# Expert routing of a two-layer transformer: VectorE's placing chain in single steps, its running count as a scan, and layer 2's first sorted rows transposed behind the first weight copies

## The reference, cut to what matters

```python
x = L0_attn_x                                              # (4, 512, 128) float32, 4 batches of 512 tokens
for layer in (0, 1):                                       # written out twice in the source
    sa, ca, ga, sb, cb, gb = modulation of silu(c) @ wmod  # |ga| and |gb| at least 0.25
    h = _layernorm(x) * (1 + ca) + sa
    x = x + ga * attention(h)       # layer 0: causal, 16 heads of 8
                                    # layer 1: full attention, then two rounds over past states, then a gate
    h = _layernorm(x) * (1 + cb) + sb
    x = x + gb * experts(h)
# experts of layer 0: top 1 of 8
logits = einsum('btd,ed->bte', xn, gate_w);  top1_idx = argmax(softmax(logits));  top1_score = max(softmax(logits))
for e in range(8):
    h = silu(xn @ W1[e] + b1[e]);  ye = h @ W2[e] + b2[e];  out = where(top1_idx == e, ye, out)
out = out * top1_score
# experts of layer 1: top 2 of 8
logits = xf @ Wg;  top_v, top_i = top_k(logits, 2);  top_w = softmax(top_v)
y[e] = (silu(xf @ W1[e]) * (xf @ W3[e])) @ W2[e]           # e = 0..7, 512 hidden columns
out = y[top_i[:, 0]] * top_w[:, 0] + y[top_i[:, 1]] * top_w[:, 1]
```

## Time and profile before

| | us |
|---|---|
| median of 3 runs | 929.11 (927.58 to 929.59) |
| profiled execution | 929.22 |
| its span in the trace | 927.5 |
| PE busy | 855.9 (92%) |
| DVE busy | 741.7 (80%) |
| ACT busy | 586.8 (63%) |
| POOL busy | 279.5 (30%) |

### The profile page before, as it was taken

How to read it: one execution, slowest core, us unless ns; L and a number is a source line. 1 busy time by engine, 2 the same in 40 slices (tenths; PEclk the granted TensorE clock), 3 DMA queues, 4 the chain that set the end, 5 groups by cost and what they waited for, 6 DMA issues and landing times.

```text
span 927.5 us, 19266 instructions
## 1 busy us (share of the span) xinstructions
PE 855.9 (92%) x6883; PEld 543.1 (59%) x6883; DVE 741.7 (80%) x2162; ACT 586.8 (63%) x1277; POOL 279.5 (30%) x419
## 2 busy tenths in 40 slices
PE   8899999887878899999999999999999999989994
PEld 7556666554478874445444544445453344978993
DVE  6888888887457678988989887987989885787674
ACT  2457576655556526898889877878776685433331
POOL 6123232436411436403210110200105422445332
PEclk9899999999989999999999999999997897989997
DMA  4324410001012214700000000000080100102123
GB/s 137 107 61 140 112 46 23 21 19 43 14 42 81 56 35 155 238 1 2 2 1 2 2 1 2 1 1 2 1 273 30 43 1 9 51 24 77 53 71 106
DMA packets 47927, 48.38 MB, mean 52 GB/s; under 512 B 5606, under 2 KB 39398, under 8 KB 47576
## 3 DMA queue, kind: packets, MB, share of 16 engines
q1 hardware_dynamic: 39784, 38.03, 14.0%
q0 software_dynamic: 3296, 6.82, 2.3%
q10 hardware_dynamic: 4752, 2.30, 0.8%
HBM read 30.83 MB, written 21.02 MB: 56 GB/s over the span
## 4 chain that ended last, share of the span: by engine, by line
PE 59%; DVE 28%; POOL 4%; issue 4%; DMA 2%; ACT 2%; DVEq 0%; SPq 0%; POOLq 0%; ACTq 0%
PE pv L1728 14%; PE st L1705 9%; DVE M L2029 8%; PE ring L1696 7%; PE ring L1597 5%; PE ring L1842 4%; DVE ring L2033 4%; PE st L1597 4%; PE st L1827 3%; DVE M L2036 2%; PE ring L1658 2%; PE ring L1608 2%; PE st L1820 1%; POOL Xd L1313 1%; PE st L1835 1%
## 5 line engine op out<-in xcount | busy, mean ns | idle before, releaser
L1454 ACT ACTIVATE Et<-st 128x512 f32<-128x512 f32 (+3 forms) x768 | 374.0, 550 | 124.0 <-PE st L1705 120.1
L2036 DVE TENSOR_REDUCE M<-ring 128x1 f32<-128x512 f32 x256 | 159.6, 682 | 26.3 <-PE ring L1696 26.2
L2029 DVE TENSOR_REDUCE M<-ring 128x2 f32<-128x512 f32 x256 | 159.3, 680 | 15.9 <-PE ring L1696 15.8
L2033 DVE CUSTOM_DVE_ANT_0 ring<-ring,maskw 128x128 f32<-128x128 f32 (+3 forms) x256 | 121.3, 509 | 25.6 <-PE ring L1696 23.9
L1728 PE MATMUL pv<-Et,Va 128*32 128x256 f32 (+3 forms) x1536 | 136.4, 416 | 1.9 <-POOL Et L1268 1.9
L1696 PE MATMUL ring<-Kbd,Qa 128*128 128x128 f32 (+3 forms) x256 | 89.1, 369 | 9.0 <-DVE M L2033 5.7
L1268 POOL TENSOR_SCALAR_AFFINE_SELECT Et<-Et 128x256 f32<-128x256 f32 x128 | 53.3, 418 | 139.3 <-ACT Et L1454 137.6
L1728 PE MATMUL pv<-Et,RV 128*32 128x256 f32 x1024 | 88.7, 419 | 1.0 <-ACT PVs L1461 1.0
L1705 PE MATMUL st<-Qb,Kbd 128*128 128x512 f32 (+3 forms) x256 | 84.5, 351 | 5.0 <-ACT Et L1454 5.0
L1696 PE MATMUL ring<-RKT,Qa 32*128 32x512 f32 x256 | 80.8, 517 | 5.1 <-DVE M L2029 3.4
L1705 PE MATMUL st<-Qb,RKT 32*128 32x512 f32 x256 | 76.6, 523 | 0.0
(11 more groups left out here) (293 smaller groups left out, 1519.0 us busy)
## 6 DMA issues: line engine op xcount, KB each, us to landing
Xd<-Xd SPq DMA_DIRECT2D x8, 1056.0 KB, 16.0
L1W<-in_L1W SPq DMA_DIRECT2D x2, 2048.0 KB, 12.3
Kbd<-Ksb SPq DMA_DIRECT2D x60, 64.0 KB, 2.0
Xs<-Xd SPq DMA_DIRECT2D x39, 66.0 KB, 1.9
W<-in_L0W SPq DMA_DIRECT2D x8, 258.0 KB, 3.8
W<-in_L0W SPq DMA_DIRECT2D x8, 256.0 KB, 4.2
G<-Zd SPq DMA_DIRECT2D x8, 256.0 KB, 4.6
Yd<-Yt ACTq DMA_DIRECT2D x30, 64.0 KB, 1.5
```

The source lines that it names most:

```text
L1454: e.activation(Et[s // 2 % 4][:, j % 2, q0:512], bank(ph)[:, q0:512], ACT.Exp, scale=SCALE).then_inc(exp_done, 1)
L2029: e.tensor_reduce(M[i][:, t, j, :], bank(ph)[:, :].rearrange("p (two n) -> p two n", two=2), AX.X, ALU.max).then_inc(mx_red, 1)
L2033: e.tensor_tensor_reduce(bank(ph)[:, 0:n], bank(ph)[:, 0:n], maskw[:, 512 - n:512], 1.0, -3e38, ALU.add, ALU.max, M[i][:, t, j, 0:1]).then ...
L2036: e.tensor_reduce(M[i][:, t, j, 0:1], bank(ph)[:, 0:n], AX.X, ALU.max).then_inc(mx_red, 1)
```

## The change

1. Routing is cut into single-instruction phases. In the parts (layer 0, q=0), (layer 0, q=1) and (layer 1, q=0) a step is left between them, so that they alternate with VectorE's other work; in the other parts they follow each other as before, or with what does not depend on them between. The phases `tally` to `used` become a list that is spread over the scatters' steps.
2. The running count: the copy of `tot` and the 8 (or 4) chained additions become one copy from PSUM straight into `carry` (now stored by expert, with the start value ahead of each expert's counts) and one `tensor_tensor_scan` over 72 (40) elements, with a constant `joined` that is 0 at each expert's start. A second copy takes the ranks out of PSUM, and the addition reads them from SBUF. The start value of `carry` is set in `hot`.
3. In layer 1 the pair of multiply, reduce and cast for the two choices becomes one of double size: three operations fewer in each part.
4. POOL sets the constants of the scan at its start: four small MEMSETs ahead of `onesM`.
5. Layer 1, part q=0: `route` moves from the list at half pace to the one at full pace, so its scatters stand 2 steps apart, not 4; `getx` and `meta` of the first chunk stand behind the four `getw`, not ahead of them.

In steps of the plan (a unit has 16), layer 1's part q=0 moves as follows: `hot` 440 to 443, `rank` 444 to 447, `pos` 448 to 453, the scatters from 452-480 to 455-469, `used` from 484 to 469-471, `loadx` 484 to 480, `getx` 490 to 499, the four `getw` from 490, 495, 500, 505 to 480, 485, 490, 495. In layer 0, part q=0: `rank` 228 to 233, `pos` 234 to 246, the scatters from 236-250 to 248-262, `loadx` 252 to 264 and `getx` 258 to 270; part q=1: `pos` 265 to 277, its scatters from 267-273 to 279-285, and layer 0's first `getw` stay at 271, 276 and 281.

```diff
     def route(l, q):
+        busy = 1 if l + q < 2 else 0
         for i in range(l + 1):
-            for part in ("top", "topi"):
-                do(part, l, q, i)
-                yield from wait(1 if q < 2 else 0)
+            for k in range(6 if i < l else 5):
+                do("top", l, q, i, k)
+                yield from wait(busy or (q < 2 and k in (1, 4)))
         do("hot", l, q)
+        yield from wait(4 if busy else 2 if q < 2 else 1)
+        do("rank", l, q)
         yield from wait(2 if q < 2 else 1)
-        for part in ("rank", "pos") if l else ("rank", "tiles", "room", "pos"):
-            do(part, l, q)
-            yield from wait(2 if q < 2 else part in ("rank", "pos"))
-            if l and part == "rank":
-                do("wts", l, q)
+        do("carry", l, q)
+        if l:
+            do("wts", l, q, 0)
+        yield from wait(busy)
+        do("ranked", l, q)
+        if l:
+            do("wts", l, q, 1)
+        yield from wait(busy)
...
+        for k in range(2):
+            do("place", l, q, k)
+            if l:
+                do("wts", l, q, 2 + k)
+            yield from wait(busy)
+        do("pos", l, q)
+        yield from wait(2 if q < 2 else 1)
...
+        pace = 1 if busy else -(-len(chain) // (TILES_OF[q] * SPREAD[l][q]))
         for n in range(TILES_OF[q]):
             do("scatter", l, q, n)
-            if l and n < 4:
-                do(("tally", "scan", "choose", "eid")[n], l, q)
-            yield from wait(SPREAD[l][q])
...
+            for _ in range(SPREAD[l][q]):
+                for ph in chain[:pace]:
+                    do(*ph)
+                del chain[:pace]
+                yield
+        for ph in chain:
+            do(*ph)
+            yield
...
     def first_tokens(l):
...
-        yield from wait(6)
-        do("getx", l, 0)
-        if l:
-            do("meta", 0)
+        if l == 0:
+            yield from wait(6)
+            do("getx", l, 0)
         while ("shifted", l, LAST_USE[l]) not in flags:
             yield
         for n in range(NF if l else LEAD):
             yield from wait(5 if n else 0)
             do("getw", l, n)
+        if l:
+            yield from wait(4)
+            do("getx", l, 0)
+            do("meta", 0)
...
-    prep += [(at["rows", 0], token_rows(1, 0)), (at["route", 0], in_turn(token_rows(1, 1), route(1, 0))),
-             (at["weights"], layer1_weights()), (at["past"], past_prep())]
+    prep += [(at["rows", 0], token_rows(1, 0)), (at["weights"], layer1_weights()), (at["past"], past_prep())]
...
+                                 (at["route", 0], in_turn(slow(token_rows(1, 1)), route(1, 0))),
...
                 if what == "begin":
                     e.memset(half, -0.5)
+                    for n in (4, 8):
+                        e.memset(joined[n][:, :, 0:1], 0.0)
+                        ins = e.memset(joined[n][:, :, 1:n + 1], 1.0)
+                    ins.then_inc(z_joined, 1)
                     e.memset(onesM[:, :], 1.0).then_inc(z_ones, 1)
...
-                    step(e.tensor_copy(r["tot"][:, :, :], bank(ph)[:, 8 * nt:16 * nt].rearrange("p (n e) -> p n e", e=E)))
...
-                    for n in range(nt):
-                        settle()
-                        step(e.tensor_tensor(r["carry"][:, n + 1, :], r["carry"][:, n, :], r["tot"][:, n, :], ALU.add))
-                    settle()
-                    e.tensor_tensor(r["rank"][:, :, :], bank(ph)[:, 0:8 * nt].rearrange("p (n e) -> p n e", e=E),
-                                    r["carry"][:, 0:nt, :], ALU.add).then_inc(dve_took, 1)
+                    step(e.tensor_copy(r["carry"][:, :, 1:nt + 1], bank(ph)[:, 8 * nt:16 * nt].rearrange("p (n e) -> p e n", e=E)))
+                    e.tensor_copy(r["rank"][:, :, :], bank(ph)[:, 0:8 * nt].rearrange("p (n e) -> p n e", e=E)).then_inc(dve_took, 1)
+                elif what == "carry":
...
+                    settle()
+                    step(e.tensor_tensor_scan(sums8, joined[nt][:, :, :].rearrange("p e n -> p (e n)"), sums8, 0.0, ALU.mult, ALU.add))
+                elif what == "ranked":
...
+                    step(e.tensor_tensor(r["rank"][:, :, :], r["rank"][:, :, :], r["carry"][:, :, 0:nt].rearrange("p e n -> p n e"), ALU.add))
...
-                        for i in range(l + 1):
-                            step(e.tensor_tensor(r["cmp"][:, :, :], rank[:, :, :], r[f"hot{i}"][:, :, :], ALU.mult))
-                            settle()
-                            step(e.tensor_reduce(r["posf"][:, :], r["cmp"][:, :, :], AX.X, ALU.add))
...
+                    elif what == "place" and k == 0:
+                        step(e.tensor_tensor(r["cmps"][:, :, :, :], rank[:, :, :].unsqueeze(1).broadcast_to([128, l + 1, nt, E]),
+                                             r["hots"][:, 0:(l + 1) * nt, :].rearrange("p (i n) e -> p i n e", i=l + 1), ALU.mult))
+                    elif what == "place":
+                        step(e.tensor_reduce(r["posf"][:, :, :], r["cmps"][:, :, :, :], AX.X, ALU.add))
```

355 lines of the change are left out of this document (192 added, 163 removed).

## The result

| | before | changed |
|---|---|---|
| median, us | 932.05 (924.06 to 940.32, 20 runs) | 919.44 (916.98 to 929.32, 20 runs) |
| ratio | | 0.9874, 95% interval 0.9854 to 0.9895 |
| profiled execution, us | 929.22 | 920.29 |
| span, us | 927.5 | 918.6 |

That is 1.26% faster, 11.7 us of 932 (interval 9.8 to 13.6); the two medians differ by 12.6. The unedited changed kernel, measured again on another chip beside the kernel before, came to 0.9907 (0.9875 to 0.9940). The forecast was 921 us and −8.4; the two profiled executions differ by 8.9.

A forecast was written before the change was run, and what follows sets the result against it. The prediction took DVE to bound the routing stretch in layer 1, with PE slowed behind it by the half clock. Its terms, +0.3 − 2.2 + 0 − 3.0 − 2.8 − 0.7 = −8.4, took 929.22 to 921 us, range 915 to 929.5.

The forecast's parts named there:

- the forecast case: Whole kernel: DVE's savings beside the routing reach the end and the low clock recovers; −8.4 us to 921, chance 0.50.
- What bounds the stage: Layer 1's three units beside routing q=0, 692.92 to 733.80: DVE sets the 40.88 us, busy 39.74, PE 36.28.
- The wait at 732.92 is a late load: Layer 1's first transposes: PE's 1.93 us wait, credited to M, was taken as late loads of sorted rows.
- The low stretch behind it goes: Unit behind, 733.80 to 751.53: the 6.80 us half-clock spell, costing 3.4, goes; −2.8 us net, between 0 and −2.8.
- Layer 1's units, −3.0: Layer 1, q=0, up to 733.80: DVE loses 2.1 us, 2.8 with the rank wait, rounded to −3.0; between 0 and −5.5.
- Layer 0, −2.2: Layer 0's routing, q=0 and q=1: half of the 4.4 us PE waits for DVE; between 0 and −4.4.
- fewer waits for masked maxima: Layer 0: the changed profile should show fewer PE waits for masked maxima, which were 2.1 and 1.8 us; no size given.
- Start, +0.3: Program start: four small MEMSETs on POOL delay layer 0's first normalization by 0.3 us, between 0 and 0.8.
- Last epilogue, −0.7: Last part's exposed chain: `pos` 0.9 us earlier gives −0.5, `used` −0.2; −0.7 in all, between 0 and −1.4.
- Rival 1, only removed operations pay: All routing: single steps save nothing, each operation keeps its 0.20 us; −3.8 us, 925.4, chance 0.13.
- Rival 2, the clock moves: PE-bound work: the 6.80 us low-clock spell appears elsewhere instead of going; −5.6 us, 923.6, chance 0.15.
- Rival 3, slower, from 0.21 us an operation: Routing units: spread operations hold every M back, deciding from 0.21 us each in layer 1's q=0; +6.3 us, 935, chance 0.12.

The follow-up runs named there:

- getx_early: Changed kernel with layer 1's first transposes and `meta` again ahead of the four weight copies: 924.73 us, ratio 0.9927 to the kernel before.
- fused_again: Kernel before plus the fusions alone (no steps between operations, half pace and early transposes kept), second measurement: 927.10 us, ratio 0.9945.
- after_again: The changed kernel unedited, measured again on another chip against the kernel before: 920.85 us, ratio 0.9907.
- l1_blocks: Changed kernel without the steps between operations in layer 1's part q=0, which also moves `rank` and the `tally` to `used` chain: 921.47 us, ratio 0.9913.
- adds_again: Changed kernel with the chained additions back in place of the scan, second measurement: 920.46 us, ratio 0.9891 to the kernel before.
- no_steps: Changed kernel without any steps between operations in both layers; fusions, full pace and late transposes kept: 924.89 us, ratio 0.9954.

## Why the prediction was right

The time, 919.4, lies within 915 to 929.5, and the forecast case, DVE bounding the routing units and the clock recovering behind them, is what happened. That it lies so near 921 is partly luck. The forecast set out from 929.11, the median of three executions, where that of twenty was 932.05, and the change was 11.7 us (9.1 to 10.0 at equal clock) and not 8.4. And the −8.9 of the profiles is near −8.4 only because misses cancel: layer 0 and the five units of layer 1 gave 5.9 us more than forecast, the other stages 5.4 less. Point by point:

- *What bounds the stage.* Supported. VectorE's busy time over the five units fell from 66.1 to 62.9 us and PE's idle time there from 4.9 to 2.0. But 5.6 of the 8.4 us there are busy time of PE and not waiting; the low clock is in it with a share that isn't settled, and the prediction counted only the second low stretch.
- *The wait at 732.92 is a late load.* Shown by its own trace (the load lands 0.13 us before the transposes start) and by getx_early and fused_again, whose waits of 4.0 and 2.9 us are credited to the load. What was not seen: the wait grows when what is ahead gets faster, so putting the transposes back costs more in the changed kernel than moving them brought alone (no gain seen, on the chip that took 945.6 us).
- *The low stretch behind it goes.* Shown in the changed trace (1.00 in place of 0.82) and in every trace with late transposes, where this unit takes 13.95 to 14.03 us at 1.00; −3.8 for −2.8 forecast. The first stretch went too in the changed trace, but one of 6.8 to 10.2 us stands in the units ahead in after_again, l1_blocks and adds_again.
- *Layer 1's units, −3.0.* Measured −4.7 in one profile, of which the three units 40.88 to 39.23 are −1.65 and the unit ahead −3.0. The shares were in the wrong place: the forecast summed what VectorE loses in the three units (2.1 us; busy 39.74 to 37.89, 1.85) and took only 0.7 us of wait for the rank block ahead of `QK`, although its 2.1 us leave the unit ahead. VectorE is busy 1.8 us less there, and the unit is 3.0 shorter, part of it PE's work that moved into the three units.
- *Layer 0, −2.2.* The mis-sized term: −5.5. It lies beyond the forecast's own bound of −4.4. The forecast halved the 4.4 us that PE waits in the three units; but PE's idle time over the stage fell by 4.0 us, 2.0 by the fusions and 1.8 by the steps, so nearly the whole of it came, and 1.5 us of busy time besides. The sign "fewer waits for masked maxima" came at the transposes alone (2.1 to 0); the others are 2.1 us, 1.8 before. What the steps did apart from moving the transposes is open.
- *Start, +0.3.* +0.21 by the rows of POOL. The +0.97 of the profile goes with the low stretch at 21.7 us.
- *Last epilogue, −0.7.* The last part's chain from its first copy to `pos` took 2.80 us, 3.33 before, so −0.5 and not −0.9:

```profile
816.50 0.18 DVE L2259 COPY carry<-ring 128x32 f32<-128x32 f32 x1
...
816.72 0.24 DVE L2267 TENSOR_TENSOR_SCAN carry<-joined,carry 128x40 f32<-128x40 f32 x1
817.42 0.17 DVE L2417 TENSOR_SCALAR wts<-wts 128x4 f32<-128x4 f32 x1 [0.46 <-DVE carry L2267]
...
819.30 0.17 DVE L2405 CAST pos<-posf 128x8 uint32<-128x8 f32 x1
```

```profile
838.88 0.63 PE L1650 MATMUL ring<-ident,Xs 128*128 128x128 f32 x4 [1.64 <-DMA Xs<-Xd]
```

  The operation behind the last scan starts 0.70 us after it began, for a reason that isn't shown; in l1_blocks, no_steps and fused_again it is 0.35. PE waits 1.64 us for the last rows, more than the 1.15 of the earlier trace rows, where less was forecast. In the traces with as much low clock as before the rest is 0.5 to 1.3 us shorter (174.6 to 175.4 against 176.0), near the forecast; the changed profile's +1.2 has 6.8 us more of low clock.
- *Rival 1, only removed operations pay.* Half of it held: the fusions alone gave 5 to 7 us, more than its 3.8. Single steps add 4.4 by no_steps (3.2 at equal clock), in which the transposes' place in layer 0 is contained. In the changed kernel 59 operations of layer 1's q=0 cost VectorE about 9.1 us (12.4 less 3.3), 0.154 each in place of 0.185.
- *Rival 2, the clock moves.* It happened beside the forecast: a stretch of 10.2 us at the low clock stands at 342.5 in the changed profile, where before there was none, and goes with the 2.3 us of the first units of layer 1: the traces without it take 28.1 us there (before, adds_again), those with it 30.4. Six of the eight variants on chips without the stalls described below have it as well. Whether the change brings it isn't shown.
- *Rival 3, slower, from 0.21 us an operation.* The price was 0.154, clear of that.

## What to carry to other kernels

A wait at a consumer that is credited to the engine ahead may be a late transfer; look up when the transfer lands. If it is late, a gain ahead of it can only make the wait longer, as here from 1.9 to 2.9 and 4.0 us, so move the consumer together with the gain. Where VectorE waits for its own last result in a chain, fuse first and then alternate the rest with unrelated long work: here the second took about as much waiting from PE in layer 0 as the first (1.8 and 2.0 us), and less in layer 1. Size single edits in the trace over fixed stages, by the idle time of the engine that bounds as well as by their length, and set executions with equal time at the low clock beside each other before a difference of 2 or 3 us is given a cause.
